# Last stage of a four-layer fp32 attention kernel: rounds of six positions in place of four, FFN started among the last passes

## The reference

```python
x = L0(x, ctx)                  # layer norm, cross attention, 16 heads of 8, weights quantised to three values
x = L1(x, ctx, masks)           # self attention, cross attention, FFN 128-512-128 with gelu; a layer norm after each
x = L2(x, ctx)                  # text/vision fusion: pooled vision vector, gate, residual, layer norm
x = L3(x, ctx, mask)            # below

def L3(hidden, kv, mask):
    h, kv_n = rmsnorm(hidden) * ln1, rmsnorm(kv) * ln1
    q, k, v = h @ Wq, kv_n @ Wk, kv_n @ Wv        # 16 query heads of 64, 4 key/value heads
    q, k = rope(q), rope(k)
    attn = softmax(q @ k.T / 8 + mask) @ v
    hidden = hidden + attn @ Wo
    y = rmsnorm(hidden) * ln2
    return hidden + (silu(y @ Wgate) * (y @ Wup)) @ Wdown
```

## Time and profile before

| quantity | value |
|---|---|
| timed runs, median (lowest to highest) | 581.41 us (581.2 to 584.8) |
| profiled execution, time | 584.25 us |
| its span, first to last instruction | 582.2 us |
| busy: TensorE, VectorE, ScalarE, GpSimd | 481.9, 374.5, 305.7, 250.0 us |
| first scores of the last stage | 300.1 us |
| last scores of the last stage | 530.08 us |
| mean granted TensorE clock | 0.953 |

### The profile page before, as it was taken

How to read it: one execution, slowest core, us unless ns; L and a number is a source line. 1 busy time by engine, 2 the same in 40 slices (tenths; PEclk the granted TensorE clock), 3 DMA queues, 4 the chain that set the end, 5 groups by cost and what they waited for, 6 DMA issues and landing times.

```text
span 582.2 us, 17181 instructions
## 1 busy us (share of the span) xinstructions
PE 481.9 (83%) x7014; PEld 380.1 (65%) x7014; DVE 374.5 (64%) x923; ACT 305.7 (53%) x737; POOL 250.0 (43%) x281
## 2 busy tenths in 40 slices
PE   0699999979999997797468887788888979897686
PEld 0367887757777775686346666576766857676564
DVE  5269766788777773245468695776858665763422
ACT  1177877647777775475344455535644443524421
POOL 4645633478788787689502231223213122111200
PEclk9999999989999997999689699999999989998987
DMA  9920000000000000000000000000000000000000
GB/s 299 236 107 3 2 3 3 2 2 2 3 3 3 3 3 1 1 1 2 0 1 2 2 3 1 2 1 13 1 10 2 12 2 2 10 2 11 9 3 16
DMA packets 12133, 11.43 MB, mean 20 GB/s; under 512 B 5144, under 2 KB 10136, under 8 KB 12056
## 3 DMA queue, kind: packets, MB, share of 16 engines
q1 hardware_dynamic: 11624, 9.01, 5.8%
q10 hardware_dynamic: 432, 1.32, 0.6%
HBM read 9.29 MB, written 1.05 MB: 18 GB/s over the span
## 4 chain that ended last, share of the span: by engine, by line
PE 58%; DVE 19%; issue 10%; ACT 6%; POOL 6%; DMA 1%; POOLq 0%; DVEq 0%; ACTq 0%
PE ps L436 7%; PE ps L674 5%; PE ps L450 4%; PE ps L591 4%; PE ps L613 4%; PE ps L426 4%; PE ps L418 4%; DVE wide L1228 4%; PE ps L621 2%; PE ps L663 2%; DVE mx L1292 2%; PE ps L379 2%; PE ps L575 2%; DVE p L1294 2%; PE ps L380 2%
## 5 line engine op out<-in xcount | busy, mean ns | idle before, releaser
L1452 POOL TENSOR_TENSOR probs<-p,rc 128x512 f32<-128x512 f32 x32 | 33.5, 1046 | 169.9 <-DVE rc L1303 169.9
L917 ACT ACTIVATE p<-p 128x512 f32<-128x512 f32 x32 | 20.2, 630 | 122.1 <-DVE p L1294 122.0
L1065 DVE TENSOR_REDUCE negm<-ps 128x8 bf16<-128x512 f32 x96 | 59.6, 682 | 25.3 <-PE ps L418 25.3
L1414 POOL TENSOR_TENSOR wide<-wide,cv 128x1024 f32<-128x1024 f32 x24 | 49.2, 2051 | 48.2 <-DVE wide L1044 48.2
L777 ACT ACTIVATE shared<-ps 128x512 f32<-128x512 f32 x96 | 57.4, 601 | 23.4 <-PE ps L436 21.7
L436 PE MATMUL ps<-cst,p 128*128 128x128 f32 x384 | 58.7, 276 | 0.4 <-ACT shared L777 0.4
L771 ACT ACTIVATE p<-ps 128x512 f32<-128x512 f32 x96 | 54.4, 596 | 8.3 <-PE ps L426 8.3
L1359 POOL TENSOR_TENSOR rstd<-veps,neghalf 128x2 f32<-128x2 f32 x40 | 29.0, 727 | 62.4 <-DVE veps L1089 34.9
L436 PEld LDWEIGHTS ps<-cst,p 128*128 128x128 f32 x384 | 45.2, 141 | 15.6 <-issue 8.8
L1292 DVE TENSOR_REDUCE mx<-ps 128x8 f32<-128x512 f32 x32 | 21.9, 686 | 32.7 <-PE ps L674 32.7
L575 PE MATMUL ps<-shared,wq 128*128 128x256 f32 x128 | 35.5, 413 | 7.8 <-DVE wide L1228 7.7
(11 more groups left out here) (180 smaller groups left out, 1142.7 us busy)
## 6 DMA issues: line engine op xcount, KB each, us to landing
late<-in_mask_l SPq DMA_DIRECT2D x2, 512.0 KB, 9.8
result<-x_all SPq DMA_DIRECT2D x8, 128.0 KB, 1.8
x_all<-in_x_tok SPq DMA_DIRECT2D x1, 896.0 KB, 9.7
wide<-in_ctx_t SPq DMA_DIRECT2D x1, 896.0 KB, 11.4
rv<-in_rv ACTq DMA_DIRECT2D x1, 768.0 KB, 7.2
cst<-in_cst ACTq DMA_DIRECT2D x1, 512.0 KB, 4.6
wa<-in_wa SPq DMA_DIRECT2D x1, 512.0 KB, 9.5
w<-in_w SPq DMA_DIRECT2D x2, 256.0 KB, 5.7
```

The source lines that it names most:

```text
L1065: V.tensor_reduce(negm[:, n % 4, :], ps[:, S_BANK[r], :].rearrange("p (a k) -> p a k", k=S), AX.X, ALU.max, negate=True).then_inc(sm["dve_ ...
L1414: P.tensor_tensor(r_op[:, w % 2, :, :], k_t[:, w % 2, :].unsqueeze(1).to_broadcast([128, 4, GT]), head_masks.unsqueeze(2).to_broadcast([12 ...
```

## The change

**Rounds.** `batch_step` now has six positions u. Positions 0 and 3 start a pair of sequences: both maxima and both subtractions stand first on VectorE, GpSimd divides both, and TensorE transposes the first at the next position and the second at the one after; `values3` of the pair stands at the end of that third position, no longer in the following round. The group's uses are spread anew: `out` stays one round behind, the gated FFN moves from two rounds behind to one, `md` from three to two. `ROUNDS` ends one round sooner. Before the first scores three rounds of steps run, not two and a third one after the FFN: `EARLY` now holds all of them. The rotated q is held twice (`q3x` is new, 2,048 columns), so that the next group's q can be written while this one's is read.

**FFN.** `mlp_in` of groups 0 to 2, `mlp_up` of 0 and 1, and `mlp_down` of 0 stand among the drain passes. The banks change to suit. The normalisation moves from GpSimd to VectorE (two instructions of the same form as L1209 for each group); GpSimd keeps inverse root, scale and shift. The projection of the pooled vision vector moves into passes 8 and 9.

```diff
-S_BANK, PT_BANK, A_BANK, N_BANK, SUM_BANK, FIN_BANK = (0, 1, 2, 3), (4, 5), 6, 7, 5, 3
+VIS = 8
+S_BANK, PT_BANK, A_BANK, N_BANK, SUM_BANK = (0, 1, 2, 3), (4, 5), 6, 7, 5
+UP_BANK, FIN_BANK, DOWN_BANK = ((1, 2), (3, 0)), 6, 5
...
         STEPS = (
-            (("l_in", 3), ("md", -3), ("in", 1), ("l_text", 3), ("l_back", 2)),
...
+            (("in", 1), ("out", -1), ("v", 0)),
+            (("k", 1), ("l_back", 2), ("md", -2)),
+            (("q0", 1), ("q1", 1), ("m_in", -1)),
+            (("kt", 1), ("ks", 1), ("l_in", 3), ("mg0", -1), ("mu0", -1), ("l_text", 3), ("q2", 1)),
+            (("l_gate", 3),),
+            (("mg1", -1), ("mu1", -1), ("q3", 1)),
         )
-        ROUNDS = range(-3, NG + 3)
...
+        ROUNDS = range(-3, NG + 2)
+        EARLY = {2: ((-3, 3),), 3: ((-3, 4), (-3, 5)), 4: ((-2, 0), (-2, 1)), 5: ((-2, 2), (-2, 3)),
+                 6: ((-2, 4), (-2, 5)), 7: ((-1, 0), (-1, 1)), 8: ((-1, 2), (-1, 3), (-1, 4), (-1, 5))}
...
@@ TensorE, after the last pass
+            transpose_probs(NW - 1, 3)
+            out_features(NW - 2)
+            mlp_in(0)
+            weigh_values(NW - 1)
+            mlp_up(0)
+            out_tokens(NW - 1)
+            project_out(NW - 2)
+            mlp_in(1)
+            mlp_up(1)
+            out_features(NW - 1)
+            mlp_in(2)
+            mlp_down(0)
+            project_out(NW - 1)
...
@@ TensorE, batch_step
+                if live and u % 3 == 0:
+                    scores3(n)
+                if live and u % 3 == 1:
+                    transpose3(2 * n)
+                if live and u % 3 == 2:
+                    transpose3(2 * n + 1)
+                for use in step(r, u):
                     fill(*use)
+                if live and u % 3 == 2:
+                    values3(n)
...
@@ ScalarE, batch_step, position 5
+                    if live:
+                        evac_t3(2 * n + 1)
+                    if has(2):
+                        sq3(r + 2)
+                    if has(-1):
+                        m_tanh(r - 1, 1)
+                    if has(3):
                         l2_exp(r + 3)
+                    if has(2):
+                        rms(r + 2)
...
@@ VectorE, batch_step
+                if u % 3 == 0 and live:
+                    smax3(2 * n)
+                    smax3(2 * n + 1)
+                    sum3(2 * n)
...
+                elif u == 3:
+                    if has(-1):
+                        read("mg0", r - 1)
+                    if live:
+                        sum3(2 * n + 1)
+                    if has(-1):
+                        read("mu0", r - 1)
+                    if has(1):
+                        read("q2", r + 1)
+                elif u == 4:
+                    if has(2):
+                        l2_norm(r + 2)
+                    if has(3):
+                        l2_max(r + 3)
+                else:
+                    if has(-1):
+                        read("mg1", r - 1)
+                        read("mu1", r - 1)
+                    if has(1):
+                        read("q3", r + 1)
+                    if has(2):
+                        rms_mean(r + 2)
+                    if has(3):
+                        l2_gate(r + 3)
...
@@ VectorE, FFN
                 layer_norm(lambda t: y[:, gs, t, :], g, "f_", gs)
+                dve.wait_ge(sm["f_r"], g + 1)
+                for t in range(TG):
+                    ins = V.tensor_scalar(yg[:, gs, t, :], y[:, gs, t, :], mv[:, gs, t, 0:1], rstd[:, gs, t:t + 1],
+                                          ALU.subtract, ALU.mult)
+                ins.then_inc(sm["f_yn"], 1)
...
@@ GpSimd, FFN
-                affine(sm["f_ve"], sm["f_r"], sm["f_yn"], sm["f_yg"], sm["f_x"], g, g, g % 2, "g3", "be3")
+                pool.wait_ge(sm["f_ve"], g + 1)
+                rsqrt(rstd[:, g % 2, :], veps[:, g % 2, :], TG, sm["f_r"])
                 if g + 2 < NG:
                     f_res(g + 2)
+                scale_shift(sm["f_yn"], sm["f_yg"], sm["f_x"], g, g, g % 2, "g3", "be3", yg, yg)
```

More of the change, by code:

```diff
@@ L968, in _ @@
[L968 to L978 removed]
+                n = 2 * r + u // 3
@@ L979, in _ @@
+            for g in range(2, NG):
+                gelu(g)
                 if g + 1 < NG:
```

441 lines of the change are left out of this document (249 added, 192 removed), and 3 rows, old and new, of the table STEPS.

## The result

| quantity | before | after |
|---|---|---|
| timed runs, median (lowest to highest) | 584.0 us (577.16 to 586.37, 20 runs) | 588.08 us (582.9 to 589.66, 20 runs) |
| ratio to before, 95% interval | | 1.0075 [1.0043, 1.0108] |
| profiled execution: time, span | 584.25, 582.2 us | 582.9, 581.1 us |
| first scores | 300.10 us | 310.12 us |
| last scores | 530.08 us | 544.61 us |

The change made the kernel 0.75% slower, where 2.4% less time was forecast. The profiled execution after is the fastest of its 20 runs, 5 us under their median; a second profile of the same kernel, taken later at 589.1 us, is shown further down.

What follows compares the result with a forecast made beforehand. TensorE's work was taken to bound the last stage, with 5 us of waits a round and a chain at the end. 301.1 + 231.9 + 35.2 = 568.2 us of span became 570.2 profiled, 567.4 forecast; range 550 to 583.

Steps and rivals of the forecast that it cites:

- 231.9: Rounds from first scores to second scores of round 7: 231.9 us against 230.0 before, since a group's gated FFN moves in.
- This lands the first scores at 301.1, 1 us later than before: From the passes to the first scores: moved FFN work, less GpSimd work and new early waits give 301.1 against 300.10 us.
- 32.5 us; I add 0.2: Full round of the last stage: 18.2 + 14.3 = 32.5 us, plus 0.2 for value reads, against 33.84 before.
- the named chain: Second half of a round: maxima, L2 normalisation, scale and shift, squares, gate tanh, gate and up reads, `q3` read, next scores.
- rounds near the floor: Rival: full rounds come near TensorE's floor at 29.8 us, 2.9 less each, total 555 us; chance 0.22.
- The end, 35.2 us: From the start of the last scores to the end: 2.9 + 15.3 + 3.2 + 13.8 = 35.2 us instead of 52.1, gaining 16.9.
- Of the head start and the relief 2.9 us are left: Earlier FFN work on TensorE and 12.6 us less on GpSimd bring `l_in` of group 0 to 242.3 instead of 245.20.
- counts in full: Rival: GpSimd's 12.6 us less before the first scores appears whole, first scores at 293, total 559 us; chance 0.12.
- Table loads: ScalarE loads its function table six times, not four, 2 more at 1.28 us; by the skill 2.8 us more.
- VectorE's stretch: Moved normalisation slows beside GpSimd, 0 to 5.6 us, taken as 0; as a rival 5.6 us, total 573, chance 0.06.
- Rms scaling: Rival: with 0.2 us of slack the rms scaling misses its slot, rounds reach 37 us, total 589; chance 0.10.
- It does not do what it says: Rival: early waits add up at half clock, first scores at 310, most of the end's gain eaten, 576 to 580; chance 0.08.

Runs made afterwards that it cites:

- the unread products: Changed kernel with TensorE products that nothing reads put into five waits ahead of the first scores: 582.57 us, 1.0025 of the kernel before.
- the old places: Changed kernel with the first group's early steps put back behind the FFN groups where the kernel before had them: 575.03 us, 0.9884 of the kernel before.
- two pairs of kernels: FFN's first transposes, ups and down put back behind the last projection: 564.42 to 560.41 us with early steps and tanh moved, 589.33 to 585.1 in the changed kernel.
- the old rounds: Changed FFN, drain and normalisation with the rounds, positions and early steps of the kernel before: 582.25 us, 0.9994 of the kernel before.
- the tanh first: Changed kernel with the second gate tanh ahead of the rms norm's squares on ScalarE: 574.43 us, 0.9877 of the kernel before.
- the kernel with both repairs: Changed kernel with early steps in their former places and second gate tanh ahead of squares: 564.42 us, 0.9703; with unread products in two waits 563.74 us, 0.967.

## Why the prediction was wrong

The sum was 301.1 + 231.9 + 35.2 = 568.2 us of span. The second profile of the changed kernel, which lies at its median, has 312.1 + 238.7 + 36.5 = 587.3; the first has 310.1 + 234.5 + 36.5 = 581.1.

**"This lands the first scores at 301.1, 1 us later than before" is the step that failed**: 9 to 11 us too early. Its waits were right in sum, 5.9 + 6.8 + 3.0 + 4.1 = 19.8 us worked out and 7.15 + 6.87 + 2.38 + 3.10 = 19.5 measured, in part by luck, since single ones are up to 1.3 us off. What was put at nothing is what follows a wait: the products at half clock, at least 5 to 7 us by the unread products, and rather 8 to 10, since 2.8 us of those products stood in the way themselves. The earlier trace rows held the sign of it, a clock of 0.85 at the end of the kernel before, and behind its wait of 10.89 us (284.16 to 300.10) the clock was 0.76. The same thing stood among the rivals, with first scores at 310, and was given 0.08. Of the rest, 0.9 us is `l_in`, which came later than worked out. Deeper lies the judgement that closer packing costs 1 us on balance: with the old places the first scores come at 302.9 and the time is 1.9% lower. The new places ask for each step before its chain is ready (7.15 us ahead of `l_back`, where the old place waits 1.71), and bring two more table loads.

**The full round, "32.5 us; I add 0.2": the chain was right, and its price was not.** The second half was worked out at 17.4 and measured at 17.09, bounded by the named chain and by the read of `q3`, with the scores waiting 2.2 us (2.4 worked out). At full clock the round is 32.5. But that wait is followed by half clock in two or three of four rounds, 1.4 us each, which the prediction put at nothing here too: 234.5 to 238.7 instead of 231.9, 2.6 to 6.8 us over. Moving the tanh up shows that the chain sets the round: 31.0 us. The rival of rounds near the floor came near this repair ("the tanh may be issued while the squares' x is early"); the kernel issues the squares first. The prediction saw TensorE wait 2.4 us for squares that were not needed and did not ask what a swap would give.

**The end, 35.2 us: right, 1.3 too short.** The last projection starts 17 us after the scores, not 14.5: the transposes wait 2.89 and 0.98 us for GpSimd's divisions, and the gate and up products behind them take 3.62 us where they take 1.99 ahead. From `m_in` on it took 12.7 us instead of 13.8.

**"Of the head start and the relief 2.9 us are left": wrong in what it credits.** `l_in` came at 243.2, 0.9 us from the 242.3 that was worked out, but without the head start it comes at 243.0. In two pairs of kernels the head start went with 4 us more, and behind the old rounds, with the other changes to the FFN, it gained nothing (0.9994). The prediction had itself seen that the last projection moves back and with it what GpSimd does next. The rival in which it counts in full (559) is excluded.

**Table loads: right in number and price.** Six at 1.28 us each; behind five of them the exponents or the gelu start at once, behind the sixth 0.78 us later, when VectorE has the maximum that they need. **VectorE's stretch: there, and partial.** The pair of normalisations took 1.00 us beside GpSimd's residual step in six of eight groups and 0.60 alone:

```profile
240.47 0.72 POOL L1561 TENSOR_TENSOR resb<-x_all,rv 128x256 f32<-128x256 f32 x1
240.53 1.00 DVE L1469 TENSOR_SCALAR yg<-y,mv,rstd 128x128 f32<-128x128 f32 x2 [4.12 <-POOL rstd L1485]
...
287.79 0.60 DVE L1469 TENSOR_SCALAR yg<-y,mv,rstd 128x128 f32<-128x128 f32 x2 [0.81 <-POOL rstd L1485]
```

That is 0.4 and not 0.7 us each time, 2.4 in all. The lock of the Trainium skill ("SBUF — State Buffer", Who interferes with whom) does not hold in full here by these rows: VectorE's pair starts 0.06 us behind an instruction of GpSimd of 0.72 us and is 0.40 us longer, not 0.66. In which part it reaches the end of the kernel is the open point above.

**The rivals.** Rounds near the floor (29.8 us): no in the kernel as changed, and 31.0 with one swap. Rms scaling: no, the full rounds never waited for it; that its 589 us are nearly the measured 588 is chance. *It does not do what it says* had the early stage right and 576 to 580 as its time; with the 2.6 to 6.8 us of the rounds and the 1.3 of the end it would have been 580 to 588. Two levels of time were also left out of the sum: this kernel ran at 583 or 588.5 us, and the forecast was set against one profile.

The best version is the changed kernel with the early steps in their old places, the tanh first and no head start: 560.41 us, 0.9616 [0.9583, 0.9648] of the kernel before. Its full round and its end, in the profile of 564.01 us:

```profile
388.33:419.30 30.97, 29.10 (x431) 23.34 (x431) 24.47 (x57) 17.65 (x50) 8.22 (x9) 1.00 0.02 7
526.07:562.20 36.13, 25.00 (x258) 19.83 (x254) 11.21 (x20) 8.77 (x19) 2.79 (x3) 0.86 0.03 9
```

TensorE is busy for 29.1 of 30.97 us. The end saves 16.0 us, where 16.9 were forecast. The rounds, which had lost, are 3 us shorter than before each when full, and 5.4 us from the first to the last scores (224.6 instead of 230.0).

## What to carry to other kernels

When a new order turns several short waits into one of 2 us or more, charge what follows it too: here a wait of 2.2 us on TensorE cost up to 1.5 us more in products at half clock, and one of 5.6 us 1.7 us on the next up alone (3.62 instead of 1.89). Ask of each instruction in the chain that sets a round whether the one in front of it on its engine is needed as soon; one swap on ScalarE was worth 2%. Work that is moved ahead to fill an engine's idle time must be followed to the engine that takes its result: TensorE's head start of three stretches ended in the same instruction of GpSimd at the same microsecond.

## What the runs showed of the hardware

Behind waits of TensorE of 5.61, 7.15 and 6.87 us the granted clock was 0.50, 1.2 GHz, for the next 5.7, 2.7 and 7.7 us; behind those of 2.17 us it fell in some rounds and not in others of the same execution (0.63 and 1.00 in the windows above). Unread products in a wait kept it at 1.00 in that wait and behind it in the changed kernel; in the kernel with both repairs it fell 3.5 us after the work behind the filled wait began. One program ran at two levels 5.5 us apart (583 and 588.5 us, mean clock 0.950 and 0.939 in their profiles), with equal waits; what chooses between them is not known.
